# Attention scores as row tiles, issued together ahead of the products with V and the maxima

## The chip, the cores and the metric

The kernel runs on one core of a Trainium2 chip. The metric is the device time of one execution in microseconds (us); the median of several runs is given, and one further execution was taken by the hardware profiler. The engines are TensorE (PE in the rows, its weight loads PEld), VectorE (DVE), ScalarE (ACT), GpSimd (POOL) and SyncE (SP, which starts the transfers).

## What is computed

Tokens `x` (2 sequences of 1024 tokens, 128 features) are layer-normed; to `x` are added a differential attention and a mixture of three out of eight feed-forward zones. What matters here is the attention, cut to:

```python
q = _apply_rope((x @ Wq.T).reshape(b, t, 16, 8), freqs, scale)
k = _apply_rope((x @ Wk.T).reshape(b, t, 16, 8), freqs, 1.0 / scale)
scores = jnp.einsum('bhtd,bhsd->bhts', q, k)      # q scaled and transposed before
probs = jax.nn.softmax(scores, axis=-1).reshape(b, 8, 2, t, t)
diff = probs[:, :, 0] - lam * probs[:, :, 1]
attn = jnp.einsum('bhts,bhsd->bhtd', diff, v)     # then a norm per head, and Wo
```

So there are 16 sub-heads of 8 features in each of 2 sequences, each with a 1024 x 1024 matrix of scores, and a softmax that subtracts the maximum of each query's row.

## The kernel before

All work sits in one program per engine, ordered by hand, with semaphores between the engines. First come the layer norm, the projections with the rotation, and 48 units of the feed-forward part; the first maxima of the attention are computed among those (`LEAD`, 24 units). The attention's main loop is the function `turn` on each engine, run four times (three in a hardware loop, the last written out), with 32 steps each: 128 steps.

**Groups.** The 32 pairs of sequence and sub-head are cut into 8 groups of four (`GJ`). In the tensors K and Q of a group each of the four sub-heads has a quadrant of 32 partitions: three blocks of 8 rows (the products with high and low parts of the split numbers), and in rows 24 and 25 the negated maximum, which a row of ones in K brings into the score. `K[:, par, j, :]` is zero outside the quadrant of sub-head j, so that a matmul over all 128 partitions gives sub-head j's scores alone.

**A step on TensorE** handles 128 keys by 512 queries of one group. It issues twelve matmuls with 512 columns each:

- four *scores* of the next step (line 1016, `ps<-Q,K`), into PSUM banks 0 to 3. They wait until ScalarE has taken the exponentials of the step before out of these banks (semaphore `exp_done`; ScalarE does it in two instructions of two banks each).
- four *maxima* matmuls (line 994, `ps<-K,Q`, function `max_slot`): scores the other way round, 128 queries by 512 keys, whose row maximum VectorE takes (line 683, `part_max`). They run some groups ahead of the scores. They go round a ring of three banks (`RING`, banks 4, 5 and 7): each one waits (`slot_read`) until VectorE has read the third one before it.
- four *products with V* (line 1023, `ps<-E,Vg`, function `probs_v`): 32 output columns each, side by side as column tiles, full float32, so that the trace has two instructions for each. They add up in bank 6.

The order in a step before is: first maximum, two scores, second maximum, two scores, third and fourth maximum, four products with V. Each pair of scores waits only for the exponentials of its own two banks.

Every eighth step one small transpose of the maxima follows the fourth maximum (line 981, `half_transpose`). It takes a slot of the same ring and waits for VectorE too. In steps 20 to 31 of the last turn no maxima are left; three of these steps have four small matmuls that gather the heads (line 1010). VectorE in `turn` reads two units (four banks) a step, and has two transposes, a reciprocal and small operations in some of every eight steps. The final part (norm per head, Wo, output) starts when the last products with V are done.

Of the kernel before, what the change touches and what calls it, by code (L numbers as in the profile page):

```python
# [24 lines left out]
P = 128  # L25
# [3 lines left out]
TB = SEQ // P  # L29
BANK = 512  # L30
# [8 lines left out]
QUAD = 32  # L39
# [14 lines left out]
STEPS = SEQ // BANK * TB  # L54
# [14 lines left out]
PAIR = 2 * STEPS  # L69
# [13 lines left out]
def unit_slot(v):  # L83

    return 2 * v + max(0, (v - 2) // (UG // 2))
# [10 lines left out]
def ring_bank(x):  # L96

    return LEAD_RING[x % 2] if x < LEAD_SLOTS else RING[x % 3]
# [23 lines left out]
def half_slot(hx):  # L122

    return HALF_SLOTS * hx + UG + 4
# [4 lines left out]
def build(nc, x, wqkv, wo, lam, w1, b1, w2, b2, wa, wb, consts, tables, out):  # L129
    with ExitStack() as ctx:  # L130
        def sem(name):
            return ctx.enter_context(nc.semaphore(name))

        ps = ctx.enter_context(nc.psum_tensor("ps", [P, 8, BANK], F32))
# [66 lines left out]
        def products(th):  # L201
# [7 lines left out]
        scr_out, zero_out, ones_in, kq_in, qmax_in, out_done = (  # L209
            sem("scr_out"), sem("zero_out"), sem("ones_in"), sem("kq_in"), sem("qmax_in"), sem("out_done"))  # L210
# [25 lines left out]
        st_done, exp_done, e_free, vg_done, a_out, at_done, rsum_done, u_free = (  # L236
            sem("st_done"), sem("exp_done"), sem("e_free"), sem("vg_done"), sem("a_out"),
            sem("at_done"), sem("rsum_done"), sem("u_free"))
# [603 lines left out]
        def _(pe):  # L842
            mm = nc.tensor.matmul
# [9 lines left out]
            for c in range(CHUNKS):  # L853

                pe.wait_ge(xa_done if c % CB else xn_done, FC * (c // CB + 1))
                for k in range(FC):
                    last = nc.tensor.transpose(ps[:, c, k * P:(k + 1) * P], XN[:, c * FC + k, :], ident)
# [52 lines left out]
            for b in range(BATCH):  # L910
                last = mm(ps[:, 7, 64 + b * TOP_K:64 + (b + 1) * TOP_K], cst[0:BATCH, C_SEL + b * P:C_SEL + (b + 1) * P],
                          rt[:, 48:48 + TOP_K], start=True, stop=True)
# [6 lines left out]
            for c in range(CHUNKS):  # L919
                t = slice(c * BANK, (c + 1) * BANK)  # L920
                mm(ps[:, c, :], identR[:], xnH[:, t], start=True, stop=False, skip_group_check=True)
                last = mm(ps[:, c, :], identR[:], xnL[:, t], start=False, stop=False, skip_group_check=True)
# [55 lines left out]
            def half_transpose(hx, half, slot, x):  # L978
                pe.wait_ge(neg_done, hx + 1)
                pe.wait_ge(slot_read, slot - (1 if x < LEAD_SLOTS else 2))  # L980
                nc.tensor.transpose(ps[0:16, ring_bank(x), 0:P], neg_max[:, half, :], ident).then_inc(slot_made, 1)

            def max_slot(it, o, sh, last):

                if last and 2 * PAIR * it + o >= ALL_UNITS:
                    return
                x, k, g, h = unit_slot(o), o % UG, o // UG, o // (UG // 2)
                base = PAIR_SLOTS * it
                if k == 0 and sh == 0:
                    pe.wait_ge(kq_in, 16 * (GJ + 1) * (2 * it + g + 1))  # L990
                back_to = 1 if x < LEAD_SLOTS else 2
                if x + sh > back_to:
                    pe.wait_ge(slot_read, base + x + sh - back_to)
                mm(ps[:, ring_bank(x + sh), :], Q[:, g % 2, k // GJ * P:(k // GJ + 1) * P],  # L994
                   K[:, g % 2, k % GJ, sh * BANK:(sh + 1) * BANK], start=True, stop=True).then_inc(slot_made, 1)
                if o % (UG // 2) == 1 and h and sh:
                    half_transpose(4 * it + h - 1, (h - 1) % 2, base + half_slot(h - 1), half_slot(h - 1))

            def heads_sum(c):


                b, th = c // CB, c % CB
                if c == 0:
                    pe.wait_ge(comb_done, 1)
                    pe.wait_ge(slot_read, SLOTS)
                for g in range(GB):
                    a, rows = 2 * (b * GB + g) + th, 2 * QUAD * (g % 2)
                    pe.wait_ge(u_free, 2 + a + 1)
                    o = ps[rows:rows + 2 * QUAD, HEADS_BANK[c], :].rearrange("p (k r c) -> p k r c", r=2, c=DV)
                    last = mm(o[:, :, g // 2, :], comb[:], U[:, a * HALF_U:(a + 1) * HALF_U], start=True, stop=True)  # L1010
                last.then_inc(heads_ps, 1)

            def scores(s, par, jj):
                th, st = s // TB, s % TB
                for j in (2 * jj, 2 * jj + 1):
                    last = mm(ps[:, j, :], K[:, par, j, st * P:(st + 1) * P], Q[:, par, th * BANK:(th + 1) * BANK],  # L1016
                              start=True, stop=True)
                last.then_inc(st_done, 1)

            def probs_v(s, par):  # L1020
                st = s % TB
                for j in range(GJ):
                    last = mm(ps[QUAD * j:QUAD * (j + 1), B_PV, :], Vg[:, par, st, j // 2, :], E[:, s % 2, j, :],  # L1023
                              start=(st == 0), stop=(st == TB - 1), skip_group_check=True)
                last.then_inc(e_free, 1)
# [5 lines left out]
            pe.wait_ge(res_done, 2)  # L1031
            pe.sem_inc(e_free, 2)
            scores(0, 0, 0)
            pe.wait_ge(z_out, CHUNKS)
            pe.wait_ge(res_done, CHUNKS - 1)
            scores(0, 0, 1)
            pe.wait_ge(gelu_done, UNITS)
            back(CHUNKS - 1)
            pe.wait_ge(slot_read, LEAD_SLOTS)

            def turn(it, last):
                for s in range(PAIR):
                    n, p = PAIR * it + s, s // STEPS
                    nxt = s + 1
                    ahead = not (last and nxt == PAIR)
                    o = LEAD + 2 * s

                    for jj in range(2):
                        max_slot(it, o, jj, last)
                        if ahead:  # L1050
                            if jj == 0 and nxt % TB == 0:
                                pe.wait_ge(qmax_in, 32 * (4 * it + nxt // TB + 1))
                            pe.wait_ge(exp_done, 2 * n + jj + 1)
                            scores(nxt % STEPS, (nxt // STEPS) % 2, jj)
                    for sh in range(2):
                        max_slot(it, o + 1, sh, last)
                    if last and 2 * PAIR * it + o == ALL_UNITS:
                        half_transpose(2 * GROUPS - 1, 1, SLOTS - 1, SLOTS - 1)
                    if last and s in HEADS_AT:
                        heads_sum(HEADS_AT.index(s))  # L1060
                    if s % STEPS == 0:
                        pe.wait_ge(vg_done, 2 * it + p + 1)
                    if s % TB == 0:
                        pe.wait_ge(a_out, PAIR // TB * it + s // TB + 1)
                    pe.wait_ge(exp_done, 2 * n + 2)
                    probs_v(s % STEPS, p)

            with pe.Fori(0, PAIRS - 1) as it:
                turn(it, False)
            turn(PAIRS - 1, True)  # L1070


# [84 lines left out]
```

## Time and profile before

| | us |
|---|---|
| median of 3 runs (548.25 to 549.42) | 549.23 |
| the profiled execution, own time | 547.23 |
| its span in the trace | 545.4 |
| TensorE busy | 517.8 |
| VectorE busy | 458.2 |
| ScalarE busy | 339.3 |

The span is the profiled execution from first to last instruction; what lies around it is 1.8 us. Busy time is the union of an engine's instructions. Matmuls are pipelined and overlap, and the trace gives each one about 0.4 us (some 0.6 us for the float32 ones), though the next starts after 0.23 us. A weight load (LDWEIGHTS) is a row of its own. The words in brackets at the end of a row of the timeline say how long the engine was idle ahead of it and what ended that; "issue" stands for nothing that the trace shows.

### The profile page before, as it was taken

Reading aid. Unit: us, or ns where it says so; the run is one execution under the profiler, and the core shown is the slowest. Engines: PE = TensorE matmul, PEld = TensorE weight load, DVE = VectorE, ACT = ScalarE, POOL = GpSimd, SP = SyncE. Lnnn points to the kernel's source line nnn. Section 1 sums busy time; section 2 is a strip of 40 time slices with the busy share of each in tenths; the row PEclk is TensorE's granted clock in tenths of the full one; section 3 lists DMA queues with packets and bytes.
Section 4 is the critical chain, followed back from the end, with each engine's and each line's share of the span. In section 5 each row is a group of like instructions: output and inputs, shape, how many; then the busy total and the mean of one; then the engine's idle time right before and its main releaser. Section 6 shows DMA issues by size and latency. Waiting matters only on the chain.

```text
span 545.4 us, 8613 instructions
## 1 busy us (share of the span) xinstructions
PE 517.8 (95%) x2607; PEld 295.6 (54%) x2607; DVE 458.2 (84%) x800; ACT 339.3 (62%) x424; POOL 68.8 (13%) x69
## 2 busy tenths in 40 slices
PE   6586999999999999999999999999999999999995
PEld 5564677777555554545555454555545455554333
DVE  2986778999889999999999999999999999998116
ACT  1440687666757666675766666666666666666872
POOL 3186961300000000000000000000000000000000
PEclk9697999999999999999999999999999999999999
DMA  9135526100000010020002001000200020000002
GB/s 314 53 108 199 176 100 199 55 1 2 0 2 1 13 58 2 1 70 0 1 1 67 1 0 46 23 1 0 69 1 0 2 67 3 0 2 1 2 2 77
DMA packets 11771, 23.46 MB, mean 43 GB/s; under 512 B 1490, under 2 KB 6226, under 8 KB 11618
## 3 DMA queue, kind: packets, MB, share of 16 engines
q1 hardware_dynamic: 11314, 20.34, 11.7%
q10 hardware_dynamic: 432, 2.81, 1.4%
q8 instruction: 13, 0.21, 0.2%
q14 instruction: 12, 0.10, 0.1%
HBM read 14.43 MB, written 8.39 MB: 42 GB/s over the span
## 4 chain that ended last, share of the span: by engine, by line
PE 74%; DVE 14%; DMA 4%; ACT 3%; issue 2%; POOL 1%; SPq 1%; ACTq 0%; DVEq 0%; POOLq 0%
PE ps L994 24%; PE ps L1023 23%; PE ps L1016 22%; DVE part_max L683 4%; DVE hL L722 4%; DMA X<-in_x 2%; ACT h L478 1%; PE ps L937 1%; DVE wbH L628 1%; DMA q_scr<-ropeL 1%; ACT hH L481 1%; DVE wbL L630 1%; DMA wb_raw<-in_wb 1%; PE ps L1010 1%; PE ps L862 1%
## 5 line engine op out<-in xcount | busy, mean ns | idle before, releaser
L683 DVE TENSOR_REDUCE part_max<-ps 128x1 f32<-128x512 f32 x512 | 340.1, 688 | 25.4 <-PE ps L994 22.3
L512 ACT ACTIVATE E<-ps 128x1024 f32<-128x1024 f32 x256 | 248.2, 1022 | 125.0 <-PE ps L1016 125.0
L994 PE MATMUL ps<-K,Q 128*128 128x512 f32 x512 | 193.7, 421 | 0.8 <-DVE part_max L683 0.3
L1016 PE MATMUL ps<-Q,K 128*128 128x512 f32 x512 | 161.4, 399 | 0.2 <-ACT zT L486 0.2
L994 PEld LDWEIGHTS ps<-K,Q 128*128 128x128 f32 x512 | 96.0, 188 | 119.3 <-DVE part_max L683 100.7
L1023 PE MATMUL ps<-E,Vg 128*32 128x512 f32 x1024 | 136.4, 605 | 0.6 <-ACT E L512 0.6
L1016 PEld LDWEIGHTS ps<-Q,K 128*128 128x128 f32 x512 | 94.8, 188 | 27.7 <-ACT E L512 10.3
L417 POOL TENSOR_TENSOR U<-AT,rsum 128x256 f32 (+1 forms) x15 | 9.3, 623 | 392.2 <-DVE rsum L776 392.2
L478 ACT ACTIVATE h<-ps 128x512 f32<-128x512 f32 x48 | 28.6, 595 | 38.0 <-PE ps L864 30.8
L722 DVE TENSOR_TENSOR hL<-h,hH 128x512 fp32r<-128x512 f32 x48 | 37.8, 802 | 8.0 <-ACT hH L481 8.0
L1023 PEld LDWEIGHTS ps<-E,Vg 128*32 128x32 f32 x1024 | 20.1, 108 | 44.7 <-issue 34.9
L481 ACT ACTIVATE hH<-h 128x512 fp32r<-128x512 f32 x48 | 30.3, 632 | 1.5
L937 PE MATMUL ps<-hH,wbH 128*128 128x512 f32 x48 | 19.4, 404 | 1.3 <-DVE hL L722 1.2
L862 PE MATMUL ps<-xnH,waH 128*128 128x512 f32 x48 | 19.8, 411 | 0.0
L863 PE MATMUL ps<-xnL,waH 128*128 128x512 f32 x48 | 19.4, 404 | 0.0
L864 PE MATMUL ps<-xnH,waL 128*128 128x512 f32 x48 | 19.4, 403 | 0.0
L773 DVE STREAM_TRANSPOSE AT<-A 128x256 f32<-128x256 f32 x32 | 13.7, 432 | 6.4 <-ACT A L542 6.4
L937 PE MATMUL ps<-hL,wbH 128*128 128x512 f32 x48 | 19.0, 396 | 0.0
L937 PE MATMUL ps<-hH,wbL 128*128 128x512 f32 x48 | 18.9, 394 | 0.0
L789 DVE TENSOR_REDUCE ss<-V 128x32 f32<-128x512 f32 x4 | 2.7, 675 | 18.3 <-ACT V L532 18.3
L614 DVE TENSOR_TENSOR rot<-ps,tab 128x512 f32<-128x512 f32 x16 | 10.7, 685 | 3.4 <-PE ps L864 3.4
L847 PE MATMUL ps<-Q 128*128 128x512 f32 x35 | 11.6, 501 | 1.5 <-DVE Q L568 1.5
(140 smaller groups left out, 321.9 us busy)
## 6 DMA issues: line engine op xcount, KB each, us to landing
Q<-q_scr SPq DMA_DIRECT2D x8, 512.0 KB
K<-k_scr SPq DMA_DIRECT2D x32, 96.0 KB
tab<-in_tables ACTq DMA_DIRECT2D x1, 2048.0 KB, 11.4
q_scr<-ropeL SPq DMA_DIRECT2D x4, 512.0 KB, 5.7
q_scr<-ropeH SPq DMA_DIRECT2D x4, 512.0 KB, 4.6
k_scr<-ropeH SPq DMA_DIRECT2D x4, 512.0 KB, 5.1
wa_raw<-in_wa SPq DMA_DIRECT2D x6, 256.0 KB, 3.0
wb_raw<-in_wb SPq DMA_DIRECT2D x6, 256.0 KB, 3.6
```

Source lines behind the costliest of these rows:

```text
L478: nc.scalar.activation(h[:, s % 2, :], ps[:, 6 + s % 2, :], ACT.Gelu_apprx_tanh).then_inc(gelu_done, 1)
L481: nc.scalar.activation(hH[:, s % H_BUFS, :], h[:, s % 2, :], ACT.Copy).then_inc(hh_done, 1)
L512: nc.scalar.activation(E[:, par, 2 * jj:2 * jj + 2, :].rearrange("p j t -> p (j t)"), ps[:, 2 * jj:2 * jj + 2, :].rearrange("p j t -> p (j ...
L683: nc.vector.tensor_reduce(part_max[:, half, col, sh:sh + 1], ps[:, ring_bank(x), :], AX.X, ALU.max).then_inc(slot_read, 1)
L722: nc.vector.tensor_tensor(hL[:, s % H_BUFS, :], h[:, s % 2, :], hH[:, s % H_BUFS, :], ALU.subtract).then_inc(split_done, 1)
L862: mm(o, lh, rh, start=start, stop=False)
L863: mm(o, lh, rl, start=False, stop=False)
L864: return mm(o, ll, rh, start=False, stop=stop)
L937: last = mm(ps[:, c, :], l[:, par, fs], r[:, buf, :], start=False, stop=end and f == FC - 1 and i == 2, skip_group_check=True)
L994: mm(ps[:, ring_bank(x + sh), :], Q[:, g % 2, k // GJ * P:(k // GJ + 1) * P], K[:, g % 2, k % GJ, sh * BANK:(sh + 1) * BANK], start=True, ...
L1016: last = mm(ps[:, j, :], K[:, par, j, st * P:(st + 1) * P], Q[:, par, th * BANK:(th + 1) * BANK], start=True, stop=True)
L1023: last = mm(ps[QUAD * j:QUAD * (j + 1), B_PV, :], Vg[:, par, st, j // 2, :], E[:, s % 2, j, :], start=(st == 0), stop=(st == TB - 1), skip ...
```

## The change

The scores of sub-head j now use the 32 partitions of its own quadrant in K and Q instead of all 128; the numbers are the same, since the rest of K was zero. The four of a step stand in four different row tiles of TensorE's array. And TensorE's order in a step becomes: four scores of the next step (after the exponentials of all four banks), four products with V, four maxima (and then the transpose or the heads' sums where a step has them).

```diff
             def scores(s, par, jj):
                 th, st = s // TB, s % TB
                 for j in (2 * jj, 2 * jj + 1):
-                    last = mm(ps[:, j, :], K[:, par, j, st * P:(st + 1) * P], Q[:, par, th * BANK:(th + 1) * BANK],
+                    rows = slice(QUAD * j, QUAD * (j + 1))
+                    last = mm(ps[:, j, :], K[rows, par, j, st * P:(st + 1) * P], Q[rows, par, th * BANK:(th + 1) * BANK],
                               start=True, stop=True)
                 last.then_inc(st_done, 1)
...
-                    for jj in range(2):
-                        max_slot(it, o, jj, last)
-                        if ahead:
-                            if jj == 0 and nxt % TB == 0:
-                                pe.wait_ge(qmax_in, 32 * (4 * it + nxt // TB + 1))
-                            pe.wait_ge(exp_done, 2 * n + jj + 1)
+                    if ahead:
+                        if nxt % TB == 0:
+                            pe.wait_ge(qmax_in, 32 * (4 * it + nxt // TB + 1))
+                        pe.wait_ge(exp_done, 2 * n + 2)
+                        for jj in range(2):
                             scores(nxt % STEPS, (nxt // STEPS) % 2, jj)
...
+                    probs_v(s % STEPS, p)
+                    for sh in range(2):
+                        max_slot(it, o, sh, last)
                     for sh in range(2):
                         max_slot(it, o + 1, sh, last)
...
-                    probs_v(s % STEPS, p)
```

TensorE before, one step of the last turn (`waits` names the semaphores that an instruction waits for; `x2` are like rows in a row):

```order
L994 MATMUL ps<-K,Q 128x512 [waits slot_read]
L1016 MATMUL ps<-Q,K 128x512 [waits exp_done]
L1016 MATMUL ps<-Q,K 128x512
L994 MATMUL ps<-K,Q 128x512 [waits slot_read]
L1016 MATMUL ps<-Q,K 128x512 [waits exp_done]
L1016 MATMUL ps<-Q,K 128x512
L994 MATMUL ps<-K,Q 128x512 [waits slot_read] x2
L1023 MATMUL ps<-E,Vg 32x512 [waits exp_done]
L1023 MATMUL ps<-E,Vg 32x512 x3
```

TensorE after, two steps of the last turn, the first of them with the transpose (scores are line 1017 there, the products with V line 1024):

```order
L994 MATMUL ps<-K,Q 128x512 [waits slot_read] x4
L981 MATMUL ps<-cst,neg_max 16x128 [waits slot_read,neg_done]
L1017 MATMUL ps<-Q,K 128x512 [waits exp_done]
L1017 MATMUL ps<-Q,K 128x512 x3
L1024 MATMUL ps<-E,Vg 32x512 [waits exp_done]
L1024 MATMUL ps<-E,Vg 32x512 x3
L994 MATMUL ps<-K,Q 128x512 [waits slot_read] x4
L1017 MATMUL ps<-Q,K 128x512 [waits exp_done]
```

The four maxima, which had two scores between the first and the second and two more between the second and the third, now follow one another, and the scores of the next step stand right behind the fourth maximum. The other engines' programs are unchanged.

TensorE at the end of the last turn, before, where no maxima are left:

```order
L1016 MATMUL ps<-Q,K 128x512 [waits exp_done]
L1016 MATMUL ps<-Q,K 128x512
L1016 MATMUL ps<-Q,K 128x512 [waits exp_done]
L1016 MATMUL ps<-Q,K 128x512
L1023 MATMUL ps<-E,Vg 32x512 [waits exp_done]
```

and after:

```order
L1017 MATMUL ps<-Q,K 128x512 [waits exp_done]
L1017 MATMUL ps<-Q,K 128x512 x3
L1024 MATMUL ps<-E,Vg 32x512 [waits exp_done]
L1024 MATMUL ps<-E,Vg 32x512 x3
```

The first two scores have lost their own, earlier wait: all four stand behind the exponentials of all four banks.

## Rows read from the trace of the kernel before

**Rows 1.** Windows: us; busy (count) of each engine; PEclk, DMA share, GB/s.

```profile
144.00:500.00 356.00, 356.00 (x1866) 184.72 (x1864) 329.76 (x547) 233.23 (x247) 12.06 (x20) 1.00 0.05 17
```

**Rows 2.** Chain that ended last: start us, us, what; one step.

```profile
340.20 0.99 PE ps L1023 x8
341.20 0.43 PE ps L994
341.63 0.47 PE ps L1016 x2
342.10 0.23 PE ps L994
342.33 0.47 PE ps L1016 x2
342.80 0.47 PE ps L994 x2
```

**Rows 3.** Timeline, one step: start us, us, engine, line, operation [idle before <-releaser].

```profile
322.66 0.50 PE L994 MATMUL ps<-K,Q 128*128 128x512 f32 x1
...
323.19 2.69 DVE L683 TENSOR_REDUCE part_max<-ps 128x1 f32<-128x512 f32 x4
...
324.72 0.16 PEld L1023 LDWEIGHTS ps<-E,Vg 128*32 128x32 f32 x8 [0.37 <-issue]
...
325.72 0.19 PEld L994 LDWEIGHTS ps<-K,Q 128*128 128x128 f32 x1 [0.84 <-DVE part_max L683]
```

**Rows 4.** Timeline in narrow windows of this step, PE.

```profile
324.39 0.40 PE L994 MATMUL ps<-K,Q 128*128 128x512 f32 x1
```

**Rows 5.** Timeline in narrow windows of this step, PEld.

```profile
324.75 0.13 PEld L1023 LDWEIGHTS ps<-E,Vg 128*32 128x32 f32 x4
```

**Rows 6.** Timeline in narrow windows of this step, DVE.

```profile
324.60 1.29 DVE L683 TENSOR_REDUCE part_max<-ps 128x1 f32<-128x512 f32 x2
...
325.20 0.68 DVE L683 TENSOR_REDUCE part_max<-ps 128x1 f32<-128x512 f32 x1
```

**Rows 7.** Timeline, late feed-forward part, where maxima wait for VectorE.

```profile
137.81 1.29 DVE L683 TENSOR_REDUCE part_max<-ps 128x1 f32<-128x512 f32 x2 [0.27 <-PE ps L994]
...
139.15 0.19 PEld L994 LDWEIGHTS ps<-K,Q 128*128 128x128 f32 x1 [0.41 <-DVE part_max L683]
139.26 0.19 PEld L937 LDWEIGHTS ps<-hH,wbH 128*128 128x128 f32 x1
```

**Rows 8.** Timeline, early part, PE: a matmul over all rows.

```profile
29.68 0.40 PE L864 MATMUL ps<-xnH,wL 128*128 128x512 f32 x1
```

**Rows 9.** Timeline, early part, PEld: the load for 8 rows behind it.

```profile
30.00 0.29 PEld L898 LDWEIGHTS ps<-lam_p,cst 8*128 8x128 f32 x2 [0.37 <-issue]
```

**Rows 10.** Timeline of a step with the transpose of the maxima, PEld.

```profile
306.15 0.09 PEld L981 LDWEIGHTS ps<-cst,neg_max 128*16 128x16 f32 x1 [0.29 <-DVE part_max L683]
...
306.36 0.16 PEld L1023 LDWEIGHTS ps<-E,Vg 128*32 128x32 f32 x8
```

**Rows 11.** Chain of waits, the transpose's piece in the same step.

```profile
306.31 0.13 PE ps L981
```

**Rows 12.** Timeline, last steps without maxima: two scores and the exponentials.

```profile
514.20 0.30 PEld L1016 LDWEIGHTS ps<-Q,K 128*128 128x128 f32 x2 [0.84 <-ACT E L512]
...
514.97 1.94 ACT L512 ACTIVATE E<-ps 128x1024 f32<-128x1024 f32 x2 [0.15 <-PE ps L1016]
```

**Rows 13.** Timeline, the first maximum of the last step with maxima (step 19).

```profile
498.16 0.50 PE L994 MATMUL ps<-K,Q 128*128 128x512 f32 x1
```

**Rows 14.** Chain of waits, the last products with V.

```profile
529.12 1.11 PE ps L1023 x8
```

**Rows 15.** Timeline, first step: first maximum, and second pair of scores.

```profile
144.16 0.19 PEld L994 LDWEIGHTS ps<-K,Q 128*128 128x128 f32 x1
...
145.11 0.30 PEld L1016 LDWEIGHTS ps<-Q,K 128*128 128x128 f32 x2 [0.18 <-ACT E L512]
```

**Rows 16.** Groups by line, 144 to 500 us: busy us, mean ns | idle <-releasers.

```profile
L683 DVE TENSOR_REDUCE part_max<-ps 128x1 f32<-128x512 f32 x462 | 308.0, 689 | 24.8 <-PE ps L994 21.8
```

More of the change, by code:

```diff
@@ L1046, in turn @@
                     o = LEAD + 2 * s
-                    for jj in range(2):
-                        max_slot(it, o, jj, last)
-                        if ahead:
-                            if jj == 0 and nxt % TB == 0:
-                                pe.wait_ge(qmax_in, 32 * (4 * it + nxt // TB + 1))
-                            pe.wait_ge(exp_done, 2 * n + jj + 1)
-                            scores(nxt % STEPS, (nxt // STEPS) % 2, jj)
+                    if ahead:
[3 more added lines that the diff above has]
+                        for jj in range(2):
+                            scores(nxt % STEPS, (nxt // STEPS) % 2, jj)
+                    if s % STEPS == 0:
+                        pe.wait_ge(vg_done, 2 * it + p + 1)
+                    if s % TB == 0:
+                        pe.wait_ge(a_out, PAIR // TB * it + s // TB + 1)
+                    pe.wait_ge(exp_done, 2 * n + 2)
+                    probs_v(s % STEPS, p)
+                    for sh in range(2):
+                        max_slot(it, o, sh, last)
                     for sh in range(2):
@@ L1060, in turn @@
                         heads_sum(HEADS_AT.index(s))
[L1061 to L1065, printed above, removed]
-                    probs_v(s % STEPS, p)
             with pe.Fori(0, PAIRS - 1) as it:
```

## The prediction

> **What bounds the kernel now.** I read the windows first: from 144 to 500 us, the main loop with maxima, TensorE is busy in every one of the 356 us, VectorE in 329.8, ScalarE in 233.2, and the granted clock is full [rows 1]. The chain of waits then shows that TensorE waits for nobody there. Its pieces for one step are 0.99 (products with V), 0.43 (first maximum), 0.47 (two scores), 0.23 (second maximum), 0.47 again (the repeated piece), 0.47 (third and fourth maximum): 3.06 us, or 0.234 for each matmul of 512 columns [rows 2]. The first maximum costs 0.20 more than the others. The timeline says why: the loads for the products with V start only after a gap of 0.37, and the load of the first maximum after one of 0.84, with nothing of it hidden [rows 3], while an ordinary load lies under the matmul ahead. A change between full matmuls and column tiles lets the array run empty first. So 116 steps at 3.06 us are the bound. VectorE has little room behind it: its four reads start 0.60 apart when they are ready (324.60 to 325.20) [rows 6], so 2.40 a step, and its other work is (329.8 - 308.0)/116 = 0.19 [rows 1, 16]. Below about 2.6 us a step it would be the bound.
>
> **What is saved.** Four scores cost 4 x 0.234 = 0.94 us now. As row tiles they should stream together. No large row tiles are in this trace; the nearest rows are the column tiles, eight of whose loads lie within 0.16 us and of which the second four start 0.03 after the first [rows 3, 5]. I take that: one stream and 0.03 for the spread. The other end, that they run one after another, is a rival.
>
> The trace bounds this only through column tiles. The Trainium skill (TensorE: Matmul & The Clock Gate, "Measured speedup vs the span model") gives 3.07 times for four row tiles of 512 columns. No row here shows it; by it the scores would take 0.94/3.07 = 0.31 us, 0.07 more than one stream and spread, and the total would be about 8 us above my sum.
>
> **What is added: another change of tiling.** The order is now maxima (full), scores (row tiles), products (column tiles): three changes a step where there were two. What one costs I read twice. From the start of the last full matmul to the first load of the other kind it is 324.72 - 324.39 = 0.33 [rows 3, 4]. For rows there is one small case: full matmul at 29.68, load for 8 rows at 30.00, so 0.32, with an unexplained gap ahead of it [rows 8, 9]. The load that then stands free costs 0.11 before its matmul starts (two loads follow each other by that, 139.15 and 139.26) [rows 7]. That the dearer change is free is another rival.
>
> **What is moved: the maxima wait for VectorE.** The fourth maximum needs the bank of the first one, and so VectorE's read of the first. Before, four scores lay between them and hid this; now only two maxima do. Counting from the load of the first maximum:
>
> 0.53 until VectorE starts on it (322.66 to 323.19) [rows 3]; 0.69 for its read [rows 16]; 0.05 until the waiting load starts (read ends 137.81 + 1.29 = 139.10, load 139.15) [rows 7]. So the fourth maximum's load starts at 1.27. TensorE was through with the third at 0.11 + 3 x 0.234 = 0.81; it stands for 0.57 net of the load, since the matmul starts at 1.38. Behind it are queued the scores, behind them the products, behind them the next first maximum: 1.38 + 0.33 (change to rows) = 1.71; + 0.11 (free load) + 0.03 (spread) + 0.33 (change to columns) = 2.18; + 1.00 (products, load to load, 324.72 to 325.72) [rows 3] = **3.18 us a step**.
>
> That is a closed ring: each term waits for the one ahead of it, and 0.12 longer than 3.06. The saving is there (without the stand the same sum is 2.61), but the wait takes it back. ScalarE doesn't bind: its two exponentials end 0.11 + 0.03 + 0.40 + 0.03 + 1.94 = 2.51 after the scores' load and are wanted at 3.18. VectorE has 3.18 - 2.6 = 0.6 idle in each step, which covers its transposes and reciprocal; if the step fell to 2.6 that cover would be gone.
>
> **The steps with the transpose.** It comes fifth in the ring and needs the read of the second maximum, which starts 0.60 after the first [rows 6]: 0.53 + 0.60 + 0.69 + 0.05 = 1.87 instead of 1.71. It is a column tile, so the scores now need a change behind it. From its load to the next it is 0.20 without a change (306.15 to 306.36) [rows 10]; with one I take 0.30. So 2.17 in place of 1.71, 0.46 more; before it cost 0.13 [rows 11]. 14 steps x 0.33 = 4.6 us.
>
> **First step.** The scores stand ahead of the first maximum. They wait for the exponentials until 145.11, where the maximum went at 144.16 [rows 15]: 0.95 us later.
>
> **Last steps.** From step 20 on there are no maxima. All four scores wait for both exponentials, and both exponentials for the scores: a ring of two engines. Two scores take 0.77 from load to exponential (514.20 to 514.97) [rows 12], which is 0.11 + 0.234 + 0.40 + 0.03; four row tiles take 0.11 + 0.03 + 0.40 + 0.03 = 0.57. With 1.94 for the exponentials [rows 12] and 0.05 for the release that is 2.56 a step, with the products inside. From the start of step 19 to the last products: 3.18 + 11 x 2.56 = 31.3, and 0.5 for the three squares on ScalarE that this ring doesn't wholly cover, 31.8 us. Before: 529.12 - 498.16 = 31.0 [rows 13, 14], since the heads' sums of 1 us each were on TensorE's path and now lie beside the exponentials. +0.8.
>
> **Sum.** 115 steps x 0.12 = 13.8; + 4.6 + 0.95 + 0.8 = 20.2. The profiled execution took 547.2, so 567.4; the median of the runs is 2.0 above it, so 569.4 by that. The profiled one lies just below the range of the three runs (548.25 to 549.42), and I take 568.
>
> **Rivals.**
>
> *No cost between full matmuls and row tiles.* If loads for row tiles go ahead under full matmuls, the scores start 0.234 after the fourth maximum: 1.38 + 0.234 + 0.03 + 0.33 + 1.00 = 2.97, 0.09 less than before. 115 x -0.09 = -10.4, with the other terms about -5: 544, faster. Against it speak the 0.32 and the gap of rows 8 and 9; for it, that this is a single case with an early, small matmul. 0.13.
>
> *The wait isn't there, VectorE becomes the bound.* If VectorE read the first maximum sooner than rows 3 show, or the ring let the fourth pass, the step would be 2.6: 115 x -0.46 = -53, about 496. It decides at a fourth maximum that is released before 0.81. Rows 3 and the order speak against it. 0.03.
>
> *The loads of the row tiles follow each other* by 0.11 each, as full loads do [rows 7]: 3 x 0.11 - 0.03 = 0.30 more, 3.48 a step. 115 x 0.42 = 48, and 10 with the rest: 607, slower. For it: a row tile loads 128 columns, not 32 as in rows 5. 0.12.
>
> *The change doesn't do what it says*, the row tiles stream one after another: 0.70 more, 3.88 a step: 115 x 0.82 = 94, and 14 with the rest (the last steps grow too): 657. 0.06.
>
> The forecast, the ring at 3.1 to 3.3 us a step (560 to 582), has 0.62. Something else, such as a lower clock while TensorE stands, 0.04, mostly slower.
>
> **How the numbers follow.** Predicted is the likeliest case, 568. The range takes in the neighbours on both sides, 0.62 + 0.13 + most of 0.12: 543 to 608. What measurement can tell from no change is 0.2%, 1.1 us. Faster: 0.13 + 0.03 and a little of the rest, 0.17; within, 0.03, since no case ends there; slower 0.80.
>
> **What would show it.** In the new profile: the chain of waits carries VectorE's reads of the first maximum, one a step, with TensorE idle about 0.5 ahead of the fourth; VectorE's idle time on maxima rises to some 0.6 a step; the scores' four matmuls start within 0.05 of each other, their loads 0.33 behind the last full matmul. Four starts 0.11 apart would be the third rival, 0.23 apart the last; no gap ahead of their loads the first. A step under 2.9 us, or a fourth maximum that doesn't wait, would make this wrong.

## The result and the profile after

The changed kernel takes 564.0 us (median) beside 549.3 for the kernel before: a ratio of 1.025, 95% interval 1.020 to 1.030. It is slower, by 2 to 3%. One of its four executions took 1020.8 us at a mean granted clock of 1.00, which nothing here explains; the median hardly hangs on it. The profiled execution took 564.0 us, its span is 562.2 (545.4 before).

The chain of waits of the changed kernel, one step (start us, us, what; scores are line 1017, products with V line 1024 from here on):

```profile
331.84 1.00 PE ps L1024 x8
332.84 0.44 PE ps L994
...
333.31 0.70 DVE part_max L683
...
334.05 0.49 PE ps L994
334.55 0.43 PE ps L1017 x2
```

Before, this chain held TensorE alone [rows 2]. Now 0.70 of the 3.14 us of each step is VectorE's read of the first maximum: TensorE makes it (332.84), VectorE reads it (333.31), and only then the fourth maximum starts (334.05). The scores cost 0.43 in place of 0.94.

Timeline of the changed kernel, one step (columns as in rows 3):

```profile
324.65 0.19 PEld L994 LDWEIGHTS ps<-K,Q 128*128 128x128 f32 x1 [0.76 <-DVE part_max L683]
...
325.07 0.19 PEld L1017 LDWEIGHTS ps<-Q,K 32*128 32x128 f32 x4 [0.24 <-issue]
325.08 0.50 PE L1017 MATMUL ps<-Q,K 32*128 32x512 f32 x4
325.51 0.16 PEld L1024 LDWEIGHTS ps<-E,Vg 128*32 128x32 f32 x8 [0.24 <-issue]
...
326.50 0.53 PEld L994 LDWEIGHTS ps<-K,Q 128*128 128x128 f32 x3 [0.84 <-DVE part_max L683]
...
327.04 0.69 DVE L683 TENSOR_REDUCE part_max<-ps 128x1 f32<-128x512 f32 x1 [0.65 <-PE ps L994]
```

All four loads of the scores lie within 0.19 us and all four matmuls within 0.50: they do stream side by side. They start 0.42 behind the load of the fourth maximum, with a gap (0.24, "issue") that no semaphore explains. I put it down to the change of tiling; the experiments below bear that out. From there it is 0.44 to the next loads, 0.99 to the first maximum (326.50), 0.54 to VectorE (327.04). VectorE stands 0.65 here; over the loop it is 0.52 a step (59.9 us in 115 steps, below), since its other work fills a part in some steps.

The same over the whole loop, as waits (engine, line, releaser: us in total, times, longest), 145 to 515 us:

```profile
DVE part_max L683 <- PE ps L994: 59.9, 115, 2.0
PE ps L994 <- DVE part_max L683: 36.7, 115, 0.3
```

VectorE waits for TensorE and TensorE for VectorE, 115 times each, where before VectorE's reads had waited 21.8 us in all [rows 16] and no maximum matmul had stood in this loop. The windows (columns as in rows 1) show the standing and a part that I had not forecast, the granted clock at the end:

```profile
150.00:500.00 350.00, 313.36 (x1773) 113.33 (x1773) 293.01 (x521) 219.77 (x233) 11.39 (x19) 1.00 0.06 17
...
520.00:545.00 25.00, 19.62 (x136) 5.07 (x132) 3.08 (x6) 20.75 (x24) 0.62 (x1) 0.86 0.01 2
545.00:562.00 17.00, 11.63 (x56) 6.92 (x56) 9.07 (x17) 5.34 (x9) 0.00 (x0) 0.83 0.20 62
```

The steps with the transpose, in the chain of the changed kernel:

```profile
338.11 1.00 PE ps L1024 x8
...
340.92 0.28 PE ps L981
341.20 0.44 PE ps L1017 x2
341.64 0.99 PE ps L1024 x8
```

341.64 - 338.11 = 3.53 us, 0.39 above an ordinary step, where it was 0.13 before [rows 11].

**Where the 16.8 us of span came from.** The 115 steps from the first to step 19 of the last turn: 115 x (3.14 - 3.06) = 9.2; 14 transposes x (0.37 - 0.13), since such steps are 3.51 apart as a rule, 3.4; the first step 0.95 (shown below); the last steps 1.0; the final part 0.9; and 1.6 us before the loop, in the feed-forward part that the change does not touch. Together 17.0.

### The profile page after: what moved, and what is told of

The parts are those of the page before. It is cut to its first block, busy times and chain, and to the rows that moved or that the text cites. A ratio compares the mean times of both kernels' runs of the same rounds, so it can differ in the third digit from the quotient of the medians.

```text
span 562.2 us, 8517 instructions
## 1 busy us (share of the span) xinstructions
PE 489.5 (87%) x2607; PEld 227.4 (40%) x2607; DVE 439.3 (78%) x800; ACT 337.9 (60%) x424; POOL 68.5 (12%) x69
## 4 chain that ended last, share of the span: by engine, by line
PE 55%; DVE 28%; issue 6%; ACT 4%; DMA 4%; POOL 1%; SPq 1%; DVEq 0%; ACTq 0%; POOLq 0%
PE ps L1024 21%; DVE part_max L683 19%; PE ps L994 18%; PE ps L1017 10%; DVE hL L722 4%; DMA X<-in_x 2%; ACT E L512 2%; DVE wbH L628 1%; ACT h L478 1%; DMA q_scr<-ropeL 1%; PE ps L937 1%; ACT hH L481 1%; PE ps L981 1%; DVE wbL L630 1%; PE ps L1082 1%
## 5 line engine op out<-in xcount | busy, mean ns | idle before, releaser
L683 DVE TENSOR_REDUCE part_max<-ps 128x1 f32<-128x512 f32 x512 | 319.0, 684 | 60.9 <-PE ps L994 60.9
L994 PE MATMUL ps<-K,Q 128*128 128x512 f32 x512 | 186.6, 444 | 38.0 <-DVE part_max L683 37.4
L994 PEld LDWEIGHTS ps<-K,Q 128*128 128x128 f32 x512 | 87.0, 188 | 197.4 <-DVE part_max L683 177.0
L1024 PE MATMUL ps<-E,Vg 128*32 128x512 f32 x1024 | 138.3, 612 | 1.0 <-ACT E L512 1.0
L1017 PE MATMUL ps<-Q,K 32*128 32x512 f32 x512 | 65.9, 502 | 6.0 <-ACT E L512 5.6
L1017 PEld LDWEIGHTS ps<-Q,K 32*128 32x128 f32 x512 | 25.0, 184 | 41.9 <-issue 25.1
```

The costliest lines, as they stand in the source:

```text
L683: nc.vector.tensor_reduce(part_max[:, half, col, sh:sh + 1], ps[:, ring_bank(x), :], AX.X, ALU.max).then_inc(slot_read, 1)
L1017: last = mm(ps[:, j, :], K[rows, par, j, st * P:(st + 1) * P], Q[rows, par, th * BANK:(th + 1) * BANK], start=True, stop=True)
```

## The experiments

Two theories stood against each other. **The ring**: a step is as long as the way from the first maximum through VectorE's read, the fourth maximum, the scores and the products. **The changes of tiling**: three in a step instead of two eat the saving, and the order costs nothing.

**The order alone.** The scores go over all 128 partitions again, in the new order.

```diff
-                    last = mm(ps[:, j, :], K[rows, par, j, st * P:(st + 1) * P], Q[rows, par, th * BANK:(th + 1) * BANK],
+                    last = mm(ps[:, j, :], K[:, par, j, st * P:(st + 1) * P], Q[:, par, th * BANK:(th + 1) * BANK],
```

> The new order alone: scores over all 128 partitions again, order scores, products, four maxima. Theory (the fourth maximum waits for VectorE's read of the first, 0.54 + 0.70 + 0.04 us behind the first one's load, and the scores are queued behind it): load 1.28, four scores behind it, next products' loads at 2.65, step 3.65 us, that is 3.06 of work plus about 0.6 of standing; some 59 us over the changed kernel in the main loop and 8 in the last steps, about 630 us. Rival (the three changes of tiling cost the time, the order itself is free): this kernel has only two of them and its step stays at 3.06, about 550 us.

Measured: 624.8 us, ratio 1.138 (1.134 to 1.141). Its chain:

```profile
329.28 0.44 PE ps L994
...
329.75 0.70 DVE part_max L683
...
330.49 0.50 PE ps L994
330.99 0.93 PE ps L1017 x4
331.92 0.99 PE ps L1024 x8
332.92 0.44 PE ps L994
```

The step is 332.92 - 329.28 = 3.64 (3.65 was expected). Two changes of tiling as before, the same twelve matmuls, and 0.58 us more (0.57 by the prediction's sum): the order alone costs what the standing was worked out to be. The rival's 550 us is excluded.

**Row tiles alone**, in the old order:

```diff
-                    last = mm(ps[:, j, :], K[:, par, j, st * P:(st + 1) * P], Q[:, par, th * BANK:(th + 1) * BANK],
+                    rows = slice(QUAD * j, QUAD * (j + 1))
+                    last = mm(ps[:, j, :], K[rows, par, j, st * P:(st + 1) * P], Q[rows, par, th * BANK:(th + 1) * BANK],
```

> Row tiles alone, in the old order: two changes between full matmuls and row tiles for each pair of scores. Theory (a change costs the 0.42 to 0.44 from load to load that the changed kernel shows, in the place of 0.234 for a full matmul that follows its like): 0.42 + 0.44 + 0.42 + 0.44 + 0.34 + 0.33 + 0.99 = 3.38 us a step, with no wait for VectorE; +37 us on the kernel before, about 585 us. Rival (changes between full and row tiles are nearly free, the loss comes from the order alone): 3.06 - 4 x 0.234 + 2 x 0.25 = 2.6 us a step, about 500 us.

Measured: 582.2 us, ratio 1.060 (1.057 to 1.063). Its chain, one step:

```profile
330.74 0.99 PE ps L1024 x8
331.73 0.43 PE ps L994
332.16 0.42 PE ps L1017 x2
332.58 0.42 PE ps L994
...
333.44 0.67 PE ps L994 x2
334.11 0.99 PE ps L1024 x8
```

The step is 334.11 - 330.74 = 3.37 us, 3.38 was expected. A pair of scores costs 0.43 as row tiles and 0.47 as full matmuls, and the maximum between two pairs 0.43 instead of 0.23. So a change between full matmuls and row tiles costs 0.2 us like one to column tiles. Two row tiles between two such changes lose, since the second change costs the matmul behind them 0.2 more; the four together take 0.43 in place of 0.94. Neither half of the change is good alone; the new order is there to gather the four scores, and pays for it with the wait.

**A longer read of the first maximum**, in both kernels:

```diff
                 dve.wait_ge(slot_made, slot + 1)
+                if extra:     # o >= LEAD and o % 2 == 0 and sh == 0
+                    nc.vector.tensor_reduce(shift[:, 0:1], ps[:, ring_bank(x), 0:BANK // 2], AX.X, ALU.max)
                 nc.vector.tensor_reduce(part_max[:, half, col, sh:sh + 1], ...
```

> The changed kernel, where VectorE reads half of the first bank of each step once more (256 columns into a spare column) ahead of its read proper. Nothing else changes, the result included. Theory (VectorE's read of the first maximum is a link of the ring): the step grows by the whole extra read, some 0.33 us, though VectorE is idle about 0.6 in each step: 3.47 us, about 602 us. Rival (TensorE's own work and changes make the 3.14): VectorE's idle time takes it in, no change, 564 us.

> The same extra read in the kernel before. Theory: there two pairs of scores lie between the first and the fourth maximum, the read's end moves from 1.22 to 1.55 and the fourth maximum's matmul starts at 1.73 anyway: no change, up to 0.1 us a step, 549 to 555 us. Rival (VectorE is nearly the bound in both kernels): +0.33 us a step, about 588 us.

Measured: the changed kernel goes from 564.0 to 611.2 us (602 expected), the kernel before from 548.9 to 558.6, a ratio of 1.017 (1.014 to 1.020). That is outside the 549 to 555 expected. The chain of the changed kernel with it (the reads are line 685, the extra one line 684, the products line 1027):

```profile
332.48 0.45 PE ps L997
332.93 0.02 issue
332.95 0.05 DVE shift L684
...
333.29 0.69 DVE part_max L685
```

The read proper starts 0.34 later, and the step, 3.47 (332.48 to 335.95), is longer by just that, though VectorE stands idle 0.5 us in each step: its read is a link of the ring. 116 x 0.33 is 38 of the 47 us; the rest is below. In the kernel before the step stays at 3.06, 328.40 to 331.46 for the products. Its 9.6 us are elsewhere, in rows like the last of these:

```profile
328.40 1.00 PE ps L1026 x8
331.46 1.00 PE ps L1026 x8
```

```profile
257.46 2.76 issue
```

That is a stand of VectorE where its hardware loop jumps back, in the two kernels with the extra read; in the kernel before the step there takes 3.30 us. That the longer program brings it is argued, not shown. The two steps around it take 6.36 and 4.18 us, and the one at the second such place (360.75) takes 6.35: 7.2 us more than the same three steps before. Part of this is the granted clock, which was at half for some 3 us behind the first stand (0.93 from 250 to 275 us). The other 12 steps with a transpose take about 0.23 more than before (3.41 instead of 3.19), 2.7 together: the transpose waits for the second read, which the extra one delays. In the changed kernel the steps at the first such place are 6.6, 5.2 and 4.6, at the second 6.2 and 4.5, 9.8 us more than ordinary ones; the clock fell behind both (0.66 from 275 to 290 us, 0.78 from 395 to 400). So this experiment confirms the theory by its steps; the totals hold two side effects that I had not counted.

**The fourth maximum between the scores and the products** (for all but the last step of a turn):

```diff
                             scores(nxt % STEPS, (nxt // STEPS) % 2, jj)
+                    if s:
+                        max_slot(it, o - 1, 1, last)
...
-                    for sh in range(2):
+                    for sh in range(1 + (s == PAIR - 1)):
                         max_slot(it, o + 1, sh, last)
```

> The changed kernel, with the fourth maximum of each step moved behind the next scores, ahead of the products with V (except in the last step of a turn). Theory (the wait for VectorE is hidden under the scores, for one more change of tiling): scores' loads at 0.89 after the first maximum's load, fourth maximum's load at 1.33 (released at 1.28), products' loads at 1.75, step 2.74 us; 112 steps x -0.3 and small additions: about 522 us, faster than both. Rival (changes of tiling are what costs, and there are now four): 3.14 + 0.2 = 3.3 us a step, about 585 us.

Measured: 521.0 us, ratio 0.948 (0.946 to 0.951). Chain:

```profile
331.30 1.00 PE ps L1024 x8
332.30 0.89 PE ps L994 x3
333.19 0.43 PE ps L1017 x3
333.62 0.43 PE ps L994
334.05 0.99 PE ps L1024 x8
```

Four changes of tiling, and 2.74 us a step: VectorE has left the chain of this step. Of the theories only the ring can make a kernel faster by adding a change.

**Maxima as row tiles too**, in the new order:

```diff
-                mm(ps[:, ring_bank(x + sh), :], Q[:, g % 2, k // GJ * P:(k // GJ + 1) * P],
-                   K[:, g % 2, k % GJ, sh * BANK:(sh + 1) * BANK], start=True, stop=True).then_inc(slot_made, 1)
+                rows = slice(QUAD * (k % GJ), QUAD * (k % GJ + 1))
+                mm(ps[:, ring_bank(x + sh), :], Q[rows, g % 2, k // GJ * P:(k // GJ + 1) * P],
+                   K[rows, g % 2, k % GJ, sh * BANK:(sh + 1) * BANK], start=True, stop=True).then_inc(slot_made, 1)
```

> The changed kernel, with the maxima as row tiles as well (the quadrant of their sub-head in Q and K; the numbers are the same): no change between full matmuls and row tiles is left, the order stays. Theory (the wait stays, one change goes): fourth maximum at 1.38, scores beside and behind it, the last at 1.62, products' loads at 1.95, step 2.94 us, about 541 us. Rival (the ring isn't the bound): TensorE's work is then 0.11 + 3 x 0.234 + 0.234 + 0.33 + 1.0 = 2.4 and the step falls to VectorE's 2.6, about 500 us.

Measured: 625 to 742 us in four executions, with mean clocks of 0.81 to 0.62. The time can only be read with the clock. Chain at full clock (maxima are line 995, scores 1018, products 1025):

```profile
213.13 0.70 DVE part_max L683
...
213.88 0.49 PE ps L995
214.37 0.23 PE ps L1018 x3
214.60 0.99 PE ps L1025 x8
```

The steps at full clock are 2.93 apart, the scores cost 0.23 in place of 0.43 and the wait is still there: as the ring says (2.94), to 0.01 us. The change of tiling between maxima and scores was worth 0.2. The total missed the 541 us expected, for from about 266 us on the granted clock is half:

```profile
200.00:250.00 50.00, 40.65 (x269) 13.14 (x267) 44.26 (x79) 33.87 (x37) 1.79 (x3) 1.00 0.09 29
...
300.00:350.00 50.00, 46.08 (x174) 13.28 (x170) 28.42 (x51) 20.27 (x22) 1.17 (x2) 0.50 0.06 19
```

and it stays there for some 370 us, as long as there are maxima, the step being 4.58. It was full again behind the last maximum (0.94 from 637 to 650 us), with TensorE busy 10.0 of 13 us. TensorE had been busy 40.7 of 50 us at the higher of its two levels, 2.4 GHz, against 44.7 in the same window of the changed kernel.

**The same in the old order**, which puts scores between the maxima and only the products behind the fourth:

> The kernel before with scores and maxima as row tiles, in its old order, so that the fourth maximum has the scores ahead of it and only the products behind it. Theory: fourth maximum's matmul at 1.38, products' loads at 1.71, step 2.71 us; 116 x -0.35 and small additions: about 510 us, the fastest of all. Rival (row tiles of maxima and scores don't stream beside each other): 3.06 stays, 549 us.

Measured: 516.0 us, ratio 0.939 (0.937 to 0.941), the fastest kernel of the study; 510 was expected. Its chain (line 995 maxima, 1025 products):

```profile
342.92 0.44 PE ps L995
...
343.38 0.70 DVE part_max L683
...
344.13 0.49 PE ps L995
344.62 0.99 PE ps L1025 x8
```

The next first maximum follows at 345.62, and the steps are 2.70 apart. This is the shortest ring: first maximum, its read, fourth maximum, one change, products. It is hardly longer than VectorE's own work: VectorE is busy 285.7 of the 300 us from 150 to 450, and in the steps with one of its transposes, 2.72 long, the chain goes through VectorE alone. A still shorter ring would gain little. Ahead of the loop this kernel loses 6.6 us (its first transpose in the loop belongs to a step that starts at 162.0 instead of 155.4): the maxima are row tiles among the full matmuls of the feed-forward part there, and the loads of line 862 stand 20 times for "issue" (7.0 us from 60 to 145), which before they don't. One execution had a clock of 0.93 and took 533.

**Filling the standing.** Four kernels issue the third maximum's matmul of each step more than once into its bank:

```diff
+                if o >= LEAD and o % 2 and sh == 0:
+                    mm(ps[:, ring_bank(x + sh), :], Q[:, g % 2, k // GJ * P:(k // GJ + 1) * P],
+                       K[:, g % 2, k % GJ, sh * BANK:(sh + 1) * BANK], start=True, stop=True)
                 mm(ps[:, ring_bank(x + sh), :], ...
```

In the changed kernel:

> The changed kernel with the third maximum's matmul of each step issued twice (same result). Theory (0.57 us of standing ahead of the fourth maximum is real room): 116 more matmuls of 0.234 us cost nothing, step 3.14, 564 us. Rival (TensorE's own work bounds the step): 116 x 0.234 = 27 us more, 591 us.

Measured: 564.8 us, ratio to before 1.026 (1.024 to 1.029), the time of the changed kernel, with TensorE busy 339 of 350 us instead of 313:

```profile
150.00:500.00 350.00, 339.12 (x1883) 133.73 (x1881) 293.30 (x521) 218.75 (x232) 11.41 (x19) 1.00 0.06 17
```

116 matmuls more, and not the 27 us that they would cost if TensorE's work were the bound.

In the kernel with all row tiles in the new order, once (quadrant rows in the repeat too):

> The kernel with all maxima and scores as row tiles in the new order, whose granted clock fell to half in the middle, with the third maximum's matmul of each step issued twice into its bank (same result). Theory (TensorE stands 0.57 us ahead of the fourth maximum, and the long standing is what lets the clock fall): the repeat lies in that standing, the step stays at 2.93, the clock stays at 1.00, about 541 us, much less than without the repeat (625 to 742). Rival (the clock fell for another reason, such as the use of 32 rows only): the clock falls again, and the time is as long as without.

Measured: 552.5 us once, at a mean clock of 0.98, and 679 to 681 three times, at one of 0.71. The expectation failed: the clock fell in most executions. (The 552 us are 11 above my figure; a step with the transpose takes 3.52 us there, in the place of 2.93, and I had left those 14 steps out, 14 x (0.59 - 0.13) = 6.4 us. Most of the rest lies ahead of the loop, as in the kernel above: the step with the first transpose starts at 165.0 us in the profiled execution, 159.7 in the changed kernel.) The window of the profiled one shows how little the repeat had added:

```profile
200.00:220.00 20.00, 16.93 (x119) 5.82 (x116) 18.25 (x34) 13.09 (x15) 1.17 (x2) 1.00 0.06 21
```

So, four times in all:

> All row tiles in the new order, the third maximum's matmul of each step issued four times (same result). With one repeat the clock had still fallen in 3 of 4 executions; but that repeat streamed beside the first two maxima in another row tile, so TensorE's busy time had hardly grown (16.9 of 20 us, from 16.4). Three repeats in one row tile take 0.85 us in a row and fill the standing ahead of the fourth maximum, which can't start before 1.28. Theory (time in which nothing streams lets the clock fall): step 2.93, clock 1.00 in every execution, about 552 us, the time of the one undisturbed execution. Rival (matmuls over 32 rows don't hold the clock, however dense): it falls again in most executions, 620 us and more.

Measured: eight of eleven executions at 547.8 to 550.1 us (median of all 549.1), three with a lower clock (562, 575 and 758). Window:

```profile
200.00:220.00 20.00, 19.85 (x130) 8.15 (x130) 18.20 (x33) 13.11 (x15) 1.18 (x2) 1.00 0.02 8
```

With the standing filled the clock falls more seldom, but not never, and the kernels with and without the fill ran on different chips, which I did not keep apart. Both theories were half right; what else lets it fall stays open. One thing the rows add: in both profiled executions in which it fell in the loop of this order, with no repeat and with one, it fell at the step that ends the first turn (3.65 us long instead of 3.51, at about 266 us). In the kernel with three repeats that step is as long (260.73 to 264.39), and the clock held. And with the fill in the old order:

> All row tiles in the old order (the fastest so far, 516 us, with one of four executions at 533 and a clock of 0.93), with the same three repeats of the third maximum. There the third maximum starts at about 0.6 and TensorE stands 0.3 ahead of the fourth; 4 x 0.234 from 0.45 on ends at 1.4, the fourth may start at 1.38: step 2.70 to 2.80. Theory: no execution with a low clock, 515 to 527 us. Rival (repeats cost what they stream, 3 x 0.234 a step): about 590 us.

Measured: 521.7 us, ratio 0.946 (0.941 to 0.950), with one of five executions at 541 and a clock of 0.93, where none was expected. The steps are 2.70 to 2.84 apart with the repeats, 3 us more over the loop, and 2.5 us come ahead of it. The repeats don't keep the clock in every execution either: the kernel without them is the better one.

**The end filled.** Three matmuls into an unused bank in each of steps 23 to 27 of the last turn of the changed kernel:

```diff
+                    if last and 22 < s < 28:
+                        for _ in range(3):
+                            mm(ps[:, 7, :], Q[:, 1, 0:P], Q[:, 1, 0:BANK], start=True, stop=True)
```

> The changed kernel with three matmuls into an unused bank in each of steps 23 to 27 of the last turn, where TensorE stands 1 us a step and waits for ScalarE; the granted clock was 0.86 from 520 to 545 us there and 0.83 behind it. Theory (the standing lets the clock fall, and the half clock costs 3 x 0.3 us there and about 1 us in the last products): the clock stays at 1.00 to the end, 562 us, 1.8 less than the changed kernel. Rival (the fall has no part in the time): 564 us, or more by the added matmuls.

Measured: 563.7 us, 0.4 below the changed kernel, which the intervals don't part; 1.8 less was expected. The window does show the clock held up to 545 us:

```profile
520.00:545.00 25.00, 22.18 (x159) 7.20 (x155) 3.08 (x6) 21.27 (x24) 0.62 (x1) 1.00 0.01 2
```

The steps there are 2.54 apart throughout (529.44 to 531.98 for the scores), instead of 2.83 at half clock. That the standing let the clock fall in these steps is shown; its share of the time, 0.9 us (31.0 from the scores of step 19 to the last products, 31.9 in the changed kernel), is seen in the profile only. In the final part the clock fell all the same (0.85 from 545 to 562 us), so that nothing came back there.

## Why the prediction was right

The forecast was 568 us, the result is 564, in the likeliest case and by its mechanism. Step by step:

- *The bound and the saving.* Four row tiles stream together with a small spread: shown by the rows of the changed kernel. Where no change of tiling stood ahead of them (maxima as row tiles too) the four scores added 0.23 us to the chain, against 4 x 0.234 before. The side sum in the prediction by the page's figure was off: 0.31 is 0.04 more than one stream and spread (0.234 + 0.03), not 0.07, and would have given 5 us, not 8. Nothing else hangs on it.

The Trainium skill (TensorE: Matmul & The Clock Gate, "Measured speedup vs the span model") has 3.07 times for four row tiles, which would be 0.31 us. The trace does not agree with it here: it is 0.23 without a change of tiling ahead and 0.43 with one.

- *The third change of tiling.* I took 0.33 from the change to column tiles [rows 3, 4], with one small case for rows [rows 8, 9], and a free load of 0.11 [rows 7]. The changed kernel shows 0.42 from the fourth maximum's load to the scores' (0.44 by my terms) and 0.44 on to the products' (0.47). Right, and together 0.05 too long.
- *The wait.* First maximum's load to VectorE 0.54, read 0.70, release 0.04; I had 0.53, 0.69, 0.05. The fourth maximum's load stands at 1.28 instead of 1.27. The closed sum was 3.18, measured 3.14. Both halves of the change alone, the longer read and the repeats confirm that this ring, and not TensorE's work, sets the step.
- *The transposes.* Forecast 0.33 more for each, measured 0.24. The transpose starts where I had it (340.92 is 1.88 behind the first maximum's load, 1.87 forecast); the scores' load follows 0.20 behind it (341.12), as without a change [rows 10], where I took 0.30.
- *The first step.* The scores' loads stand at 146.72, where the first maximum stood at 144.16 before: 2.56 later. Of this, 1.6 came from the part ahead (its last matmul is at 143.81 instead of 142.18); the rest, 0.95, is as forecast.
- *The last steps.* From the scores of step 19 (513.04) to the last products (545.01) it is 31.97, forecast 31.8. It came out by luck: the squares on ScalarE cost less, and three steps at half clock cost 0.3 us each:

```profile
529.66 1.94 PE L1024 MATMUL ps<-E,Vg 128*32 128x512 f32 x8
531.76 0.80 PE L1017 MATMUL ps<-Q,K 32*128 32x512 f32 x4 [0.17 <-ACT E L512]
```

- *What the sum lacked.* The clock, named only among the rest at 0.04, cost about 1 us in the last steps. The final part is 0.9 longer, at 0.83 where it was 1.00 before; that the clock is all of that is argued, not shown. And the 2.0 us between the profiled execution and the median of before did not come again: of the changed kernel the profiled one took 564.03, the median is 564.00. The sum of 20.2 was 3.4 us too high: 4.6 by 0.04 us in each step and 1.3 by the transposes, less the 0.9 of the final part and the 1.6 ahead of the loop.

The rival "no cost between full matmuls and row tiles" is excluded by the row tiles alone; "the wait isn't there" by the order alone; loads one after another and streams one after another by the rows of the changed kernel.

## What to carry to other kernels

When work is moved together, look at what lay between it: a matmul that goes round a ring of banks waits for the reader of the bank, and whatever was hiding that wait has to stay between them. Write the closed way from an operation back to itself with its own durations; where it is longer than each engine's work, more speed on one engine gives nothing, and moving one instruction out of the way can give much (here 564 to 521 us, 8%). Row tiles pay where several stand together and where no change of tiling is put ahead of them: here that meant making the neighbours row tiles too.

## What the runs showed of the hardware

- A change between full matmuls and row tiles cost 0.2 us here, the same as one to column tiles (0.43 in place of 0.23 for the matmul behind it), also where nothing but the tiling changed. Behind the small transpose no such cost showed (0.20 to the next load). The four loads of the row tiles lie within 0.19 us, the length of one.
- The granted clock fell to its lower level, 1.2 GHz, while TensorE was busy 41 of 50 us, and stayed there for some 370 us though the rows then show it busy 46 of 50. With the idle time filled this was rarer (three of eleven executions instead of four of four), so that a kernel with 348 more matmuls takes 549 us where the one without takes 625 to 742. What lets the clock fall in the remaining executions I can't say.
- VectorE with the longer program stood for 2.8 us and 2.9 us where the hardware loop jumps back (issue, at 257.46 and 360.75), in a kernel in which its work otherwise was mostly hidden. Why is not shown.
